# Layers 0 and 1 of a graph network: node rows turned in squares by VectorE and moved inside SBUF in place of TensorE transposes, with the edge blocks' work three pairs behind

## The reference

```python
# layer 0
diff = x[dst] - x[src]
max_diff = segment_max(diff, dst); max_diff = where(isneginf(max_diff), 0, max_diff)
x1 = layernorm(x + relu(concatenate([x, max_diff], axis=1) @ W + b))
# layer 1, a node without incoming edges (agg1 = agg2 = 0)
xx = silu(x1 @ lin_W.T + lin_b)
h1 = silu((agg1 @ rel1_W.T + rel1_b + xx @ root1_W.T) @ lin1_W.T + lin1_b)
h2 = silu((agg2 @ rel2_W.T + rel2_b + xx @ root2_W.T) @ lin2_W.T + lin2_b)
h = concatenate([h1, h2], axis=1) @ cat_W.T + cat_b + xx
for i in range(3):
    h = silu(h @ lins_W[i].T + lins_b[i]) + h
# then a graph norm over all nodes, a last product, layers 2 and 3
```

## Time and profile before

| | |
|---|---|
| median of 3 runs | 5533.62 us (5523.48 to 5541.32) |
| profiled execution | span 5523.1 us; the page gives no other time for it |
| TensorE busy | 4551.3 us, 82% of the span |
| VectorE, ScalarE, GpSimd busy | 4178.7, 3700.6, 4058.2 us |
| stage `nodes01` | from the first transposes at 30 us to the first of the next stage at 2024 us |
| DMA | 1084.50 MB, 196 GB/s over the span |

### The profile page before, as it was taken

How to read it: one execution, slowest core, us unless ns; L and a number is a source line. 1 busy time by engine, 2 the same in 40 slices (tenths; PEclk the granted TensorE clock), 3 DMA queues, 4 the chain that set the end, 5 groups by cost and what they waited for, 6 DMA issues and landing times. The chain is left out here.

```text
span 5523.1 us, 86293 instructions
## 1 busy us (share of the span) xinstructions
PE 4551.3 (82%) x20518; PEld 2819.0 (51%) x20518; DVE 4178.7 (76%) x8262; ACT 3700.6 (67%) x9029; POOL 4058.2 (73%) x4123
## 2 busy tenths in 40 slices
PE   7999999999999999999999999999677756661000
PEld 4566666666666644444444477777455534451000
DVE  5766666666666658888888899999788854457776
ACT  4777777777777754444444488888688864446665
POOL 6777777777777768777777477777777767777777
PEclk9999999999999999999999999999855555665555
DMA  4556656556565646555555599999799867775443
GB/s 121 142 140 135 136 139 139 139 139 140 139 140 135 140 112 195 178 179 179 176 180 176 170 356 367 365 367 365 270 291 287 276 208 228 230 236 163 134 137 103
DMA packets 558505, 1084.50 MB, mean 196 GB/s; under 512 B 131183, under 2 KB 225065, under 8 KB 558279
## 3 DMA queue, kind: packets, MB, share of 16 engines
q1 hardware_dynamic: 452918, 931.29, 54.7%
q0 software_dynamic: 100352, 149.23, 11.2%
q10 hardware_dynamic: 5008, 1.60, 0.1%
HBM read 648.47 MB, written 438.76 MB: 197 GB/s over the span
## 5 line engine op out<-in xcount | busy, mean ns | idle before, releaser
L832 ACT ACTIVATE p_s<-p_ps,cols 128x512 f32<-128x512 f32 x588 | 404.5, 688 | 317.3 <-PE p_ps L774 207.7
L685 POOL DMA_INDIRECT p_xs<-in_x,src_cols x388 | 376.4, 970 | 221.1 <-DVE p_r L900 131.5
L1163 POOL DMA_INDIRECT ring_rows<-t_rows,home_cols x384 | 446.8, 1164 | 120.4 <-issue 88.6
L692 POOL DMA_INDIRECT home<-edge_row_cols,scatter_cols x392 | 414.8, 1058 | 131.2 <-issue 119.2
L182 POOL DMA_INDIRECT out<-u_res,scatter_cols x392 | 407.2, 1039 | 121.8 <-issue 117.8
L175 POOL DMA_INDIRECT u_rows<-t_rows,home_cols x392 | 388.6, 991 | 145.6 <-issue 118.5
L175 POOL DMA_INDIRECT ring_rows<-t_rows,home_cols x400 | 396.7, 992 | 128.2 <-issue 115.2
L685 POOL DMA_INDIRECT p_xd<-in_x,dst_cols x388 | 391.4, 1009 | 107.5 <-issue 89.0
L1172 POOL DMA_INDIRECT home_cols<-home,src_cols x376 | 379.8, 1010 | 111.4 <-issue 85.9
L1259 ACT ACTIVATE q_s<-q_ps,cols 128x512 f32<-128x512 f32 x294 | 202.1, 687 | 355.9 <-PE q_ps L1236 310.7
L900 DVE TENSOR_TENSOR p_r<-p_s,p_r 128x512 f32<-128x512 f32 x392 | 267.9, 683 | 194.0 <-ACT p_s L832 192.5
(11 more groups left out here) (310 smaller groups left out, 14446.8 us busy)
## 6 DMA issues: line engine op xcount, KB each, us to landing
p_x<-in_x SPq DMA_DIRECT2D x98, 512.0 KB, 6.5
t_rows<-p_o SPq DMA_DIRECT2D x98, 512.0 KB
hT<-ring_own SPq DMA_DIRECT2D x98, 512.0 KB
q_hn<-hT SPq DMA_DIRECT2D x98, 512.0 KB
r_h<-hT SPq DMA_DIRECT2D x98, 512.0 KB
r_x<-t_rows SPq DMA_DIRECT2D x98, 512.0 KB
t_rows<-r_y SPq DMA_DIRECT2D x98, 512.0 KB
t_rows<-r_x SPq DMA_DIRECT2D x98, 512.0 KB
```

The lines of the kernel that those rows point to most:

```text
L685: nc.gpsimd.indirect_dma_start(out=rows[:, j, :], out_offset=None, in_=a["x"], in_offset=bass.IndirectOffsetOnAxis(ap=idx[:, j:j + 1], axi ...
L692: nc.gpsimd.indirect_dma_start(out=tab["home"], out_offset=bass.IndirectOffsetOnAxis(ap=s["scat"][:, k:k + 1], axis=0), in_=s["at"][:, k:k ...
L832: nc.scalar.activation(act_out[i][:, :], flat(bank_r), ACT.Silu, bias=col(LS0 + i)).then_inc(r_act[i], 1)
L1163: nc.gpsimd.indirect_dma_start(out=rows[:, e % 4, j, :], out_offset=None, in_=tab["t1"], in_offset=bass.IndirectOffsetOnAxis(ap=s["home"][ ...
```

## The change

`o` is no longer transposed by TensorE and copied by ScalarE. VectorE turns it in squares into a new tile `o_turned` (`turn_squares`, in step t+3), and SyncE moves the squares inside SBUF with 16 DMAs of 32 partitions by 256 elements for a pair of blocks (`swap_groups`), into `x1T`. The `lin` product reads `x1T` in runs of 32 elements (`by_column`). `lin` and all that follows on it comes three steps later than before: `lin` at t+6, `R1`/`R2`/`cat` at t+7, the residual rounds at t+8, the last add at t+9. The edge blocks' work is 3 pairs behind the node pair (`BEHIND`), not 1. The stage has 206 steps, not 202. Counts and lags in the waits follow.

```diff
+def swap_groups(sp, across, turned, sem):
+    for a in range(4):
+        for c in range(4):
+            sp.dma_start(across[32 * c:32 * (c + 1), a], turned[32 * a:32 * (a + 1), c]).then_inc(sem, DMA)
+def by_column(across):
+    return across.rearrange("p a (j i) -> p j a i", j=G)
...
-        xT, x1T, xx = sb("p_xT", [P, 2, BLK]), sb("p_x1T", [P, 2, BLK]), sb("p_xx", [P, 4, BLK])
+        xT, xx = sb("p_xT", [P, 2, BLK]), sb("p_xx", [P, 4, BLK])
+        o_turned, x1T = sb("p_oT", [P, 2, 4, 2, P]), sb("p_x1T", [P, 2, 4, 2, P])
...
-        QB = EB + 1
-        STEPS = 2 * QB + 4
+        BEHIND = 3
+        QB = EB + BEHIND
+        STEPS = NB + 10
...
+        def counted_by(q):
+            if not q.fixed:
+                return 3 * q.b + 3 - BEHIND
+            return min(2 * q.b + 2, NB) + min(max(q.b - BEHIND + 1, 0), EB)
         @block.sync
...
-                e = t // 2
+                e = t // 2 - BEHIND + 1
                 if e >= 2 and live(e, EB):
                     after(sp, scanned, e - 1)
...
-                e = (t - 8) // 2
+                e = (t - 8) // 2 - BEHIND + 1
...
-                n = t - 10
+                n = t - 12
                 if live(n, NB):
                     sp.wait_ge(r_added[2], n + 2)
                     sp.dma_start(tab["hT"][n // 2].rearrange("p (h c) -> p h c", h=2),
                                  hs[3][:, slots(n), :]).then_inc(h_saved[n // 2 % 2], DMA)
+                n = t - 6
+                if live(n, NB):
+                    q = n // 2
+                    sp.wait_ge(o_squared, n + 2)
+                    after(sp, lined, n - 2)
+                    swap_groups(sp, x1T[:, q % 2], o_turned[:, q % 2], x1_in[q % 2])
         @block.gpsimd
...
-                e = t
+                e = t - BEHIND + 1
                 if live(e, EB):
                     map_rows(e, range(0, 2))
-                    after(pool, r_added[0], 2 * e - 5)
+                    after(pool, r_added[0], 2 * t - 8, NB)
         @block.tensor
...
             def step(t):
-                e = t.pair().back(1)
+                e = t.pair().back(BEHIND)
...
-                n = t.back(5)
+                n = t.back(8)
                 if n.live(NB):
                     pe.wait_ge(r0_ready, n.b + 1)
...
-                n = t.back(3)
-                if n.live(NB):
-                    pe.wait_ge(applied, n.b + 1)
-                    if t.live(NB):
-                        pe.wait_ge(x_copied, t.b + 1)
-                    else:
-                        bank_t_left(t)
-                    transpose4(nc, bank_t, o[:, n.of(4)], s["ident"]).then_inc(x1_turned, 1)
...
-                n = t.back(3)
+                n = t.back(6)
                 if n.live(NB):
-                    pe.wait_ge(x1_copied, n.b + 1)
+                    q = n.pair()
+                    pe.wait_ge(x1_in[q.of(2)], landed(2, q, 16))
                     after(pe, h1_ready, n.b)
-                    nc.tensor.matmul(flat(bank_l), s["lin"][:, :], x1T[:, n.of(2), :],
+                    nc.tensor.matmul(flat(bank_l), s["lin"][:, :], by_column(x1T[:, q.of(2), :, n.slot % 2]),
                                      start=True, stop=True).then_inc(lined, 1)
         @block.scalar
...
-                n = t.back(3)
-                if n.live(NB):
-                    act.wait_ge(x1_turned, n.b + 1)
-                    after(act, lined, n.b - 1)
-                    nc.scalar.activation(x1T[:, n.of(2), :], flat(bank_t), ACT.Copy).then_inc(x1_copied, 1)
         @block.vector
...
-                n = t.back(6)
+                n = t.back(9)
                 if n.live(NB):
                     residual(2, n)
-                n = t.back(5)
+                n = t.back(3)
+                if n.live(NB):
+                    q = n.pair()
+                    dve.wait_ge(applied, n.b + 1)
+                    if n.past(4):
+                        dve.wait_ge(x1_in[q.of(2)], landed(2, q.back(2), 16))
+                    turn_squares(nc, o_turned[:, q.of(2), :, n.slot % 2].rearrange("p c (j i) -> p c j i", j=G),
+                                 o[:, n.of(4)]).then_inc(o_squared, 1)
+                n = t.back(8)
                 if n.live(NB):
                     residual(0, n)
```

More of the change, by code:

```diff
@@ L583, in nodes01 @@
         squares_saved, e_squared = [sem(f"squares_saved{i}") for i in range(2)], sem("e_squared")
-        (x_turned, x_copied, x1_turned, x1_copied, product, biased, summed, counted, guarded, rooted, scaled,
+        o_squared, x1_in = sem("o_squared"), [sem(f"x1_in{i}") for i in range(2)]
+        (x_turned, x_copied, product, biased, summed, counted, guarded, rooted, scaled,
          applied, lined, active, u_done1, u_done2, h1_ready, h2_ready, cat_done, r0_ready) = (sem(m) for m in (
-             "x_turned", "x_copied", "x1_turned", "x1_copied", "product", "biased", "summed", "counted",
+             "x_turned", "x_copied", "product", "biased", "summed", "counted",
              "guarded", "rooted", "scaled", "applied", "lined", "active", "u_done1", "u_done2", "h1_ready", "h2_ready",
@@ L601, in batch @@
             lo = 0 if q.live(EB) else 2 * G
-            return lo, C if q.back(1).live(EB) else 2 * G
+            return lo, C if q.back(BEHIND).live(EB) else 2 * G
+        def counted_by(q):
+            if not q.fixed:
+                return 3 * q.b + 3 - BEHIND
+            return min(2 * q.b + 2, NB) + min(max(q.b - BEHIND + 1, 0), EB)
         block = ctx.enter_context(nc.Block())
@@ L733, in bank_t_left @@
             def bank_t_left(t):
-                e = t.back(1).pair().back(1)
+                e = t.back(1).pair().back(BEHIND)
                 if t.slot % 2 == 1 and e.live(EB):
                     pe.wait_ge(xd_copied, e.b + 1)
-                elif t.back(4).live(NB):
-                    pe.wait_ge(x1_copied, t.back(4).b + 1)
                 elif t.back(1).live(NB):
@@ L755, in step @@
                                      start=True, stop=True).then_inc(r_done[0], 1)
-                n = t.back(4)
+                n = t.back(7)
                 if n.live(NB):
@@ L806, in step @@
                     pe.wait_ge(xd_in[e.of(2)], landed(2, e, G))
-                    if t.back(3).live(NB):
-                        pe.wait_ge(x1_copied, t.back(3).b + 1)
-                    elif t.live(NB):
-                        pe.wait_ge(x_copied, t.b + 1)
-                    else:
-                        bank_t_left(t)
+                    after(pe, x_copied, t.b + 1, NB)
+                    if t.fixed and t.b >= NB:
+                        pe.wait_ge(xd_copied, e.b)
                     transpose4(nc, bank_t, xd[:, e.of(2)], s["ident"]).then_inc(xd_turned, 1)
-                n = t.back(5)
+                n = t.back(8)
                 if n.live(NB):
@@ L863, in step @@
                         act.wait_ge(saved[q.of(2)], landed(2, q.back(2)))
-                        act.wait_ge(x1_turned, n.b - 3)
+                        act.wait_ge(o_squared, n.b - 3)
                     scale_shift(nc, o[:, n.of(4)], v[:, n.of(4)], rs[:, q.of(2), c:c + G],
                                 nm[:, q.of(2), c:c + G]).then_inc(applied, 1)
-                e = t.pair().back(1)
+                e = t.pair().back(BEHIND)
                 if even and e.live(EB):
@@ L872, in step @@
                 q = t.pair().back(1)
-                e = q.back(1)
+                e = q.back(BEHIND)
                 if even == (t.fixed and t.b >= NB) and e.live(EB):
@@ L935, in step @@
                     stats_of(nc, st[:, q.of(2), c:c + G], v[:, n.of(4)]).then_inc(counted, 1)
-                n = t.back(5)
+                n = t.back(8)
                 if n.live(NB):
                     residual(1, n)
-                n = t.pair().back(3)
+                n = t.pair().back(BEHIND + 2)
                 if even and n.live(EB):
```

18 lines of the change are left out of this document (9 added, 9 removed).

## The result

The changed kernel takes 5501.32 us (median of 4 runs, 5489.46 to 5503.65) against 5529.73 us for the kernel before, run beside it (4 runs, 5523.48 to 5541.32): a ratio of 0.9946, 95% interval 0.9931 to 0.9961. It is 28 us faster where 75 were forecast; it lies inside the widest range given (5436 to 5515) but outside the forecast's own (5440 to 5485), in the direction given. The profiled run took 5502.12 us.

A forecast was written before the change was run, and what follows sets the result against it. TensorE's own work was taken to bound the stage. Transposes -85 us, VectorE wait +10, fill -4, drain +4 sum to -75 us: 5459 us (-1.4%), own range 5440 to 5485, chance 0.64.

The forecast's parts named there:

- the widest range given: Whole-kernel time of 5436 to 5515 us, stretched towards the case of new TensorE waits to leave out at most 2 in 10.
- TensorE sets the stage, and 196 x 0.435 us of transposes go: Changed stage: TensorE busy 200 of 200 us; removing the transposes of `o` saves 85 us.
- The tight chain: VectorE in an even step, bias add to end of `CAT_B` add, 5.24 us: TensorE waits 0.1 us a pair, 10 us.
- The turn: VectorE turns `o` in squares, 0.70 us a block, in an idle stretch before the first residual add; delays nobody.
- the strided read: `lin` reading its columns in runs of 32: no cost, as an edges1 product reading squares took 592 ns.
- GpSimd is not the bound: Steady pair: GpSimd's own chain 17.8 us against a new pair of 19.15, so 1.3 us to spare.
- 16 swaps take 7.6 us: SyncE's 16 DMAs of 32 KB a pair, 0.47 us each like the squares' loads, landing 6 us before `lin`.
- rival 2: Swaps become the bound at `lin`'s wait if 16 issues exceed 13.8 us; at 1.0 us each, 5666 us; chance 0.09.
- Fill -4, drain +4: Stage start gains 4 us (-8 to +12) from less idle TensorE; stage end loses 4 us (0 to +12).
- Later stages as long as before: Stages after the changed one, from the first transposes of edges1 on: no change in length expected.
- Rival 1: TensorE waits in each pair in more than one chain, losing about half of 0.87 us: 5499 us; chance 0.20.
- Rival 3: Transposes were hidden, so the pair stays near 19.95 us: within 17 us of before, 5530 us; chance 0.07.

## Why the prediction was right and wrong

- *TensorE sets the stage, and 196 x 0.435 us of transposes go*: right. TensorE stays at 199.98 of 200 us at clock 1.00, and the same even step lacks the four transposes of `o`.
- *The tight chain costs 98 x 0.1 = 10 us*: right in kind, 0.165 us a pair and so 16 us (0.27 and 0.06 in turn). The pair saves 0.71 us, 69 us in 98 pairs, instead of 75. The 0.1 did not come out of its own figures: 1008.00 + 0.1 for the signal against 1008.09 is 0.01 us. No row gave the 0.1 for the signal (0.05 measured). The wait comes from the other pair of the loop, which was not read: there the chain of the kernel before ends at 1028.14, and 1028.14 + 0.05 against 1028.02 is the 0.17 us that was measured.
- *The turn takes 0.70 us in an idle stretch; the strided read costs nothing; GpSimd is not the bound*: right. 704 ns median; `lin` 592 ns; GpSimd still waits 7.8 and 2.2 us for VectorE between 1000 and 1200 us, about 1.0 us a pair (1.3 forecast).
- *16 swaps take 7.6 us*: wrong, 10.9. The row it rested on the earlier trace rows is another kind of transfer, 64 KB from memory; which difference makes the issue dearer was not tested. In the steady part the 6 us of slack took it up. The margin for rival 2 was overstated: its limit for the burst, 13.8 us, is 2.9 us away and not 6.2.
- *Fill -4, drain +4*: the step that failed. It put start and end together at no loss. Measured: 40.2 saved at the stage end, against 69 in the pairs, so 29 us lost. Of these 11.7 at the start, 6.4 in two waits for swaps at the end, and 6.9 more idle time ahead of edges1; 4 us are left, spread over fill and drain and not taken apart.
 - The sum's work for a pair without `x` is 0.8 us too high (16 units of 0.86 and 2.65 make 16.4, not 17.2), so its gaps are 1.7 us and not 0.9. For the two such pairs that were added that makes 3.4 us, near the 3 that it used: the loss does not come from there.
 - The start: the sum counted SyncE's queue only in a steady pair. The 21 copies that stand once behind the swaps were never listed, though 16 more issues ahead of them make that pair's queue 26 us long. Spreading them gave back 7.1 us.
 - The end: one us late was forecast for the pair in which the squares' loads and the swaps meet; 2.2 and 4.2 it was, as both bursts ran over 0.47 us an issue (the loads 8.7, the swaps 10.1).
 - The tail: GpSimd was asked about in a steady pair alone. At the end its last 16 gathers, 20 us, come behind a power that waits for the last edge block, and three pairs of lag leave TensorE little to do beside them. The lag of one shows that this part is not a pure loss: what it returns at the end it takes at the start.
- *Later stages as long as before*: not borne out. Of the 47 us between the forecast and the medians, 6 are the pair's and 29 those of start and end; some 12 are left behind the stage. The 17.5 us more in the first profile are mainly gathers of the last stage, 1026 against 991 ns (392 of them, 13.4 us). They come and go in the changed kernel; in the kernel before no profile shows them over 1007 ns. Why the medians meet them more often after the change is open.
- Rival 1 named 5499 us, which is where the time fell, but by another way: there is no new wait in each pair beyond the one counted. Its number is a coincidence. Rival 2 was right about its mechanism: TensorE waits for the swaps in each pair when the burst takes 16.11 us (24 DMAs), over the limit of 13.8, and not at 10.90 (16). Rival 3 fell.
- The Trainium skill (DMA: Bandwidth & Descriptors, Bandwidth) says that transfers under 64 KB are descriptor-dominated. The fixed part of about 2.0 us that the prediction added stands in another section of that page of the Trainium skill, Anatomy of one DMA, for the path that GpSimd issues. It did not decide: read in series it is an estimated 32 us a pair, 10.9 us were measured. What does add up in series is SyncE's own time for each issue, 0.66 to 0.68 us, and with 24 and 32 of them it set the pair.

## What to carry to other kernels

Where a change adds issues to a queue, walk that queue through every burst that the program has once, at the start and at the end, and not only through a steady round: the steady part took 10.9 us of new issues at no cost, and the two irregular places lost 17 us that a mere reordering gave back. Read more than one profile of each kernel, and compare the medians with what the changed stage gained: a difference between the two lies outside the stage. Price an issue by the nearest row of the same kind of transfer, and as a cost for each DMA that adds up on the issuing engine. Ask of every engine what it still has to do after the last work of the bound one.

## What the hardware showed that was not expected

- A move of 32 or 16 KB inside SBUF, issued in a burst by SyncE, takes 0.66 to 0.68 us of SyncE each (median 0.59, single ones up to 2.8 in the changed kernel), against 0.47 for loads of 64 KB from memory in the kernel before and 0.55 for the same loads in the changed kernel (8.72 us for 16). Half the bytes made no move cheaper.
- 35 GB/s more of DMA traffic changed the steady pair by 0.003 us.
- The same 392 gathers of the last stage take 985 or 1026 ns each in the changed kernel, from run to run, which moves the total by some 16 us; 984 to 1007 in three profiles of the kernel before. That is as much as the edits compared here, so the stage end in the trace told more than the medians.
- One chip ran the unaltered kernel before in 6473 us against 5524 to 5530 in the three groups elsewhere. Variants of the changed kernel show waits there that no record explains, and two of them that gain elsewhere (0.6% and 1.0%) lose 1.1 and 1.3%.
